# Attention scores from high and low parts of keys and queries, in products of 64 rows

## The chip, the core and the metric

The kernel runs on one core of a Trainium2 chip. Its time is that of one execution on the device in microseconds (us). The engines are TensorE (PE; its weight loads are listed apart as PEld), VectorE (DVE), ScalarE (ACT), GpSimd (POOL) and the queue that issues most transfers (SP). They run side by side and wait for one another through semaphores.

## What is computed

A layer with three parts runs on 8 batches of 64 rows of width 512. The first part is cross attention to a context of 1601 rows in 16 heads of width 32, with a "stablemax" in place of the softmax:

```python
def stablemax(x):
    s = jnp.where(x >= 0, x + 1.0, 1.0 / (1.0 - x))
    return s / jnp.sum(s, axis=-1, keepdims=True)
q = query @ Wq.T + bq          # and k, v from key_value
scores = jnp.einsum('bhqd,bhkd->bhqk', q, k) / np.sqrt(HD).astype(np.float32)
attn = stablemax(scores)
context = jnp.einsum('bhqk,bhkd->bhqd', attn, v)
```

Then come a causal self attention with 8 query heads and one key head, and a feed-forward part with 2 shared experts and 8 routed ones of which each row takes two. Each part adds its result to its input.

## The kernel before, in words

**Stages.** The cross attention takes most of the first 815 us. It goes batch by batch and in 104 chunks of keys, 13 to a batch: 12 of 128 keys and one of 65. The context comes in six parts to a batch (`PARTS`: five of 256 keys, one of 321), two chunks to a part and three to the last. Work is laid out by slots, one for each chunk (`for n in range(NSLOT)` in every engine's program). In a slot with an even number within its batch PE does the scores of two chunks (`group`), and then the weighted sums of the two before. In every slot it projects keys of the next part (two of its four blocks of 128 features, `keys`, L691) and the values of one chunk (`values`, L703). The self attention of finished pairs of batches ("tiles") is spread over these slots too (`STEPS`). The feed-forward part follows: shared experts to about 1015 us, then the routed ones.

**High and low parts.** The projections use fp32r operands: a value is rounded into a high part, the rest makes a low part, and three products (high by high, high by low, low by high) are summed in PSUM. The scores do not: `scores` (L719) multiplies the keys `kk` and queries `qc` in fp32, one product for each of four heads in a block g, over the 32 rows of the head: load `kk[r, ...]`, 32 rows by 128 keys, and move the 64 queries. Four products of a block lie on the four groups of 32 rows of the array and write four banks of `sc`.

**Buffers and order.** Projections take turns in two banks (`pj`). `take` lets PE write a bank only when `proj_read` says that DVE has read what lay there two uses ago. DVE's `keys` (L1234) adds the bias and stores a block, `values` (L1242) copies. DVE's order in an even slot: values of the slot before, first key block, weights of the first chunk, second key block; in the odd slot: values, weights of the second chunk, third and fourth key blocks.

**From scores to weights.** ACT reads the scores with Relu (L1133), then does Ln (L1140) and Exp (L1144); DVE's `weights` (L1247) adds the positive part, again from PSUM. POOL sums the weights for the denominators (L557) and makes the low parts of the context (L543). `weighted` (L732) multiplies weights and values in products of 128 rows by 32 columns; `denominators` (L744) sums over the rows.

**End of the stage.** SP loads the first expert weights (1 MB each, `load_shared`, L407) into a ring of buffers, three of them at slot NCH - 12, where NCH is 104; ACT rounds them (`weights_hi`, L1093), DVE makes the low part (L1338). `gelu` (L1100), `hidden` (L1347, L1349) and `shared_up` belong to the shared experts. The part's buffers (`sb1`) lie in the same memory as later ones, so that a ring buffer can be filled only when what lay there is done with.

Of the kernel before, what the change touches and what calls it, by code (L numbers as in the profile page):

```python
# [168 lines left out]
def build(nc, x, ctx0, ctx1, ctx2, ctx3, ctx4, ctx5, wq, bq, wk, bk, wv, bv, wo, bo, ak, av, aq, ap_, abp, rw, rb,  # L169
# [3 lines left out]
    with st:  # L173
# [17 lines left out]
        sd = sb("sd", [P, 4])  # L191
        rstd = sb("rstd", [P, 4])
# [60 lines left out]
        def sb1(name, shape, dt=F32):  # L253
# [9 lines left out]
        kk = sb1("kk", [P, 2, 4, WID])  # L263
        va = sb1("va", [P, VR, D])
        wqt = sb1("wqt", [P, 4, D])
        wot = wqt
        qc = sb1("qc", [P, 4, D])
        tt = sb1("tt", [P, TR, 1024])
        unit = sb1("unit", [P, 32])
# [14 lines left out]
        xBl = sb("xBl", [P, 4, 256], F32R)  # L284
        hh = sb("hh", [P, 4, D], F32R)
        hl = sb("hl", [P, 4, D], F32R)
        iota512 = sb("iota512", [P, D])
        sb("pad0", [P, 312])
        xr = sb("xr", [P, 2, D])
        GT = sb("GT", [P, 2, D], F32R)  # L290
        late_ring = [sb(f"ring{i}", [P, 2048]) for i in range(5, 8)]
        sb("pad1", [P, 32])
        ring = [sb(f"ring{i}", [P, 2048]) for i in range(3)] + early_ring + late_ring
        wsh, wsl = [sb("wsh0", [P, 2048], F32R), wsh1, wsh2], [sb("wsl0", [P, 2048], F32R), wsl1, wsl2]
        hr = sb("hr", [P, 2, D])
# [21 lines left out]
            "wkh_act wvh_act ch_act t_act ln_act ex_act rstd_act xt_act q_act "  # L317
            "exp_act xh_act gap_act wT_act ge_act wh_act rg_act yh_act "
            "pad_dve eps_dve iota_dve ones_dve wkl_dve wvl_dve cl_dve bqs_dve xr_dve proj_read f_dve "
# [49 lines left out]
        def weights_view(n, kn, hb):  # L369
            return tt[0:kn, n % TR, 512 * hb:512 * hb + 512].rearrange("p (h c) -> p h c", h=2)  # L370
# [12 lines left out]
        def sync(e):  # L383
# [31 lines left out]
            for n in range(NCH):  # L415
# [42 lines left out]

            e.wait_ge(s["v_pe"], NCH)
# [188 lines left out]
        def pe(e):  # L648
# [58 lines left out]
            def scores(n):  # L707
                i, k, kn = chunk(n)
                u, b, c0 = i % 2, i // NPT, 256 * (n - group_of(n)[0])
# [12 lines left out]

            def weighted(n):
# [6 lines left out]
                for g in range(4):  # L730
                    for h in range(4):
                        m = e.matmul(pob[b % 2][32 * h:32 * h + 32, 64 * g:64 * g + 64],  # L732
                                     va[0:kn, n % VR, P * g + 32 * h:P * g + 32 * h + 32],
                                     tt[0:kn, n % TR, 256 * h + 64 * g:256 * h + 64 * g + 64],
                                     start=(head and g == 0), stop=(tail and g == 3), skip_group_check=True)
                m.then_inc(s["p_pe"], 1)

            def denominators(b):
                dst = take("d", b)
                e.wait_ge(s["da_pool"], PER * b + PER)  # L740
                if b == 0:
                    e.wait_ge(s["unit_pool"], 1)
                for h in range(4):
                    m = e.matmul(dst[32 * h:32 * h + 32, 0:256], unit[:], dacc[:, b % 2, 256 * h:256 * h + 256],  # L744
                                 start=True, stop=True)
# [304 lines left out]
        def act(e):  # L1050
# [9 lines left out]

            def root(l, t):
# [62 lines left out]

            for n in range(NSLOT):
                for m in group(n):
# [4 lines left out]
                    e.wait_ge(s["s_pe"], group(n)[-1] + 1)  # L1131
                    for hb in range(2):
                        e.activation(weights_view(m, kn, hb), score_read(m, kn, hb), ACT.Relu,  # L1133
# [92 lines left out]
        def vector(e):  # L1226
            def keys(i, g):
# [16 lines left out]
            def weights(n, hb):  # L1244
                kn, t_ = chunk(n)[2], weights_view(n, chunk(n)[2], hb)
                e.wait_ge(s["ex_act"], 2 * n + hb + 1)
                e.scalar_tensor_tensor(t_, score_read(n, kn, hb), 0.0, t_, ALU.max, ALU.add).then_inc(s["f_dve"], 1)  # L1247
# [165 lines left out]
            e.tensor_copy(kio[:], iotai[:, P:P + 120].rearrange("p (k e) -> p k e", e=8)).then_inc(s["iota_dve"], 1)  # L1413
            values(0)
# [92 lines left out]
            for n in range(NSLOT):  # L1507
# [55 lines left out]
                for b, g, m in finished(n)[1]:  # L1563
                    normalised(b, g, m)

# [123 lines left out]
```

## Time and profile before

| what | us |
|---|---|
| median of 3 runs | 1291.81 (1291.58 to 1291.93) |
| the profiled execution's own time | 1291.71 |
| its span, from the first to the last instruction | 1290.0 |
| PE busy | 1278.1 |
| DVE busy | 640.0 |
| ACT busy | 625.2 |
| POOL busy | 405.8 |

The span is what the profile's rows add up to; the run's time has 1.7 us more around it. Busy times of engines overlap. In a row of the timeline the first number is the start in us from the span's start, the second the time to the end of the last of the merged instructions; "128*32" is rows by columns of the array that a product uses, and the shape after it is that of what is read. An fp32r operand that PE reads is listed as f32. An instruction's own duration holds its latency, so that durations of neighbours overlap: the pace of a row of instructions is read from their starts.

### The profile page before, as it was taken

Reading aid. Unit: us, or ns where it says so; the run is one execution under the profiler, and the core shown is the slowest. Engines: PE = TensorE matmul, PEld = TensorE weight load, DVE = VectorE, ACT = ScalarE, POOL = GpSimd, SP = SyncE. Lnnn points to the kernel's source line nnn. Section 1 sums busy time; section 2 is a strip of 40 time slices with the busy share of each in tenths; the row PEclk is TensorE's granted clock in tenths of the full one; section 3 lists DMA queues with packets and bytes.
Section 4 is the critical chain, followed back from the end, with each engine's and each line's share of the span. In section 5 each row is a group of like instructions: output and inputs, shape, how many; then the busy total and the mean of one; then the engine's idle time right before and its main releaser. Section 6 shows DMA issues by size and latency. Waiting matters only on the chain.

```text
span 1290.0 us, 31423 instructions
## 1 busy us (share of the span) xinstructions
PE 1278.1 (99%) x13820; PEld 1125.7 (87%) x13820; DVE 640.0 (50%) x971; ACT 625.2 (48%) x1093; POOL 405.8 (31%) x212
## 2 busy tenths in 40 slices
PE   8999999999999999999999999999999999999998
PEld 6898898888888889888889889798889999999897
DVE  5334443544443443443444454666776555565555
ACT  4445554544444544544543645647534444554443
POOL 1344444444444444444445435200032000100000
PEclk9999999999999999999999999999999999999999
DMA  6131111121111102121112031564566499999991
GB/s 221 61 109 34 35 38 35 34 71 53 48 63 35 46 27 99 35 74 39 35 38 100 23 127 63 237 254 164 171 193 202 151 334 352 360 343 332 359 392 39
DMA packets 34941, 174.98 MB, mean 136 GB/s; under 512 B 6184, under 2 KB 8392, under 8 KB 18544
## 3 DMA queue, kind: packets, MB, share of 16 engines
q1 hardware_dynamic: 33056, 168.16, 36.1%
q0 software_dynamic: 1744, 4.76, 1.1%
q8 instruction: 111, 1.82, 0.6%
q14 instruction: 30, 0.25, 0.1%
HBM read 166.84 MB, written 6.06 MB: 134 GB/s over the span
## 4 chain that ended last, share of the span: by engine, by line
PE 96%; DVE 2%; DMA 1%; ACT 0%; issue 0%; SPq 0%; DVEq 0%; ACTq 0%
PE bank L691 23%; PE bank L703 22%; PE bank L1017 11%; PE sc L1034 9%; PE sc L719 8%; PE sc L879 6%; PE bank L732 4%; PE bank L898 3%; PE sc L898 3%; PE bank L791 1%; PE bank L755 1%; PE bank L839 1%; DMA xres<-in_x 1%; PE bank L854 1%; PE sc L854 1%
## 5 line engine op out<-in xcount | busy, mean ns | idle before, releaser
L557 POOL TENSOR_TENSOR xn<-xn,tt 128x1024 f32<-128x1024 f32 x96 | 231.4, 2411 | 364.2 <-DVE tt L1247 363.9
L1133 ACT ACTIVATE tt<-sc 128x512 f32<-128x512 f32 (+1 forms) x208 | 108.0, 604 | 392.7 <-PE sc L719 392.7
L1338 DVE TENSOR_TENSOR wsl<-ring,wsh 128x2048 fp32r<-128x2048 f32 x72 | 167.7, 2330 | 113.3 <-ACT wsh L1093 113.1
L691 PE MATMUL bank<-cxh,wkh 128*128 128x256 f32 (+1 forms) x752 | 222.4, 296 | 1.0 <-DVE va L1242 1.0
L691 PE MATMUL bank<-cxl,wkh 128*128 128x256 f32 (+1 forms) x752 | 215.9, 287 | 0.4 <-issue 0.4
L691 PE MATMUL bank<-cxh,wkl 128*128 128x256 f32 (+1 forms) x752 | 215.1, 286 | 0.0
L1234 DVE TENSOR_SCALAR kk<-bank,bkt 128x256 f32<-128x256 f32 (+1 forms) x190 | 93.1, 490 | 202.1 <-PE bank L691 202.1
L703 PE MATMUL bank<-wvh,cxh 128*128 128x512 f32 (+1 forms) x416 | 164.5, 395 | 0.0
L703 PE MATMUL bank<-wvl,cxh 128*128 128x512 f32 (+1 forms) x416 | 163.8, 394 | 0.0
L703 PE MATMUL bank<-wvh,cxl 128*128 128x512 f32 (+1 forms) x416 | 162.8, 391 | 0.0
L1093 ACT CAST wsh<-ring 128x2048 fp32r<-128x2048 f32 x72 | 137.4, 1909 | 46.8 <-PE sc L1034 21.1
L1242 DVE COPY va<-bank 128x512 f32<-128x512 f32 (+1 forms) x104 | 71.8, 690 | 171.3 <-PE bank L703 171.3
L691 PEld LDWEIGHTS bank<-cxh,wkh 128*128 128x128 f32 x752 | 141.8, 189 | 11.0 <-issue 2.9
L1247 DVE SCALAR_TENSOR_TENSOR tt<-sc,tt 128x512 f32<-128x512 f32 (+1 forms) x208 | 133.3, 682 | 29.6 <-ACT tt L1144 29.6
L1017 PEld LDWEIGHTS bank<-xT,ring 128*128 128x128 f32 x1280 | 144.8, 192 | 1.0
L1017 PE MATMUL bank<-xT,ring 128*128 128x128 f32 x1280 | 144.8, 275 | 0.0
L691 PEld LDWEIGHTS bank<-cxl,wkh 128*128 128x128 f32 x752 | 141.9, 189 | 1.4
L691 PEld LDWEIGHTS bank<-cxh,wkl 128*128 128x128 f32 x752 | 142.3, 189 | 0.5 <-issue 0.5
L1140 ACT ACTIVATE tt<-tt 128x512 f32<-128x512 f32 (+1 forms) x208 | 121.6, 648 | 0.0
L1144 ACT ACTIVATE tt<-tt 128x512 f32<-128x512 f32 (+1 forms) x208 | 121.3, 645 | 0.0
L543 POOL TENSOR_TENSOR cxl<-ctxt,cxh 128x1024 fp32r<-128x1024 f32 (+1 forms) x47 | 108.3, 2305 | 27.5 <-ACT cxh L1059 27.5
L719 PEld LDWEIGHTS sc<-qc,kk 32*128 32x128 f32 (+1 forms) x3328 | 94.6, 182 | 20.2 <-issue 19.7
(257 smaller groups left out, 1965.4 us busy)
## 6 DMA issues: line engine op xcount, KB each, us to landing
ring<-in_w SPq DMA_DIRECT2D x112, 1024.0 KB, 7.2
ctxt<-in_ctx SPq DMA_DIRECT2D x40, 512.0 KB, 3.6
ctxt<-in_ctx SPq DMA_DIRECT2D x8, 642.0 KB, 4.0
wqt<-in_wo SPq DMA_DIRECT2D x4, 1024.0 KB, 6.5
wqt<-in_aq SPq DMA_DIRECT2D x4, 1024.0 KB, 6.2
wqt<-in_ap_ SPq DMA_DIRECT2D x4, 1024.0 KB, 5.7
yrows<-K SPq DMA_DIRECT2D x1, 2048.0 KB, 9.9
tt<-in_wk SPq DMA_DIRECT2D x2, 512.0 KB, 5.2
```

The source lines that it names most:

```text
L543: e.tensor_tensor(lo, src, hi.bitcast(F32), ALU.subtract).then_inc(s["cl_pool"], 1)
L557: e.tensor_tensor(dacc[0:kn, y, :], dacc[0:kn, y, :], tt[0:kn, w, :], ALU.add).then_inc(s["da_pool"], 1)
L691: m = e.matmul(dst[:, 0:n], (wkh, wkl)[a][:, c, g * P:(g + 1) * P], (cxh, cxl)[b][:, u, c, 0:n], start=(c == 0 and x_ == 0), stop=(c == 3 ...
L703: m = e.matmul(dst[0:kn, :], (cxh, cxl)[a][:, u, c, k * P:k * P + kn], (wvh, wvl)[b][:, c, :], start=(c == 0 and x_ == 0), stop=(c == 3 an ...
L719: m = e.matmul(sc[0:kn, h, c0 + 64 * g:c0 + 64 * g + 64], kk[r, u, g, k * P:k * P + kn], qc[r, g, 64 * b:64 * b + 64], start=True, stop=True)
L1017: m = e.matmul(bank[q % 2][:, P * jj:P * jj + P], ring[slot(un)][:, 512 * c + P * jj:512 * c + P * jj + P], xg[:, y, c, :], start=(c == 0) ...
L1034: m = e.matmul(bank[2][:], h_[:, j, :], w_[r_ % 3][:, 512 * jj:512 * jj + 512], start=(j == 0 and x_ == 0), stop=(j == 15 and x_ == 2))
L1093: e.copy(wsh[m % 3][:], ring[slot(un)][:]).then_inc(s["wh_act"], 1)
L1140: e.activation(tt[0:kn, w, r], tt[0:kn, w, r], ACT.Ln, bias=1.0).then_inc(s["ln_act"], 1)
L1144: e.activation(tt[0:kn, w, r], tt[0:kn, w, r], ACT.Exp, scale=-1.0).then_inc(s["ex_act"], 1)
L1247: e.scalar_tensor_tensor(t_, score_read(n, kn, hb), 0.0, t_, ALU.max, ALU.add).then_inc(s["f_dve"], 1)
L1338: e.tensor_tensor(wsl[m % 3][:], ring[slot(unit_split(m))][:], wsh[m % 3][:].bitcast(F32), ALU.subtract).then_inc(s["wl_dve"], 1)
```

## The change

The scores are made of three products with fp32r operands. The keys have a high part `kh` and a low part `kl`, both written by DVE from the same bank. The queries of a batch have `qh` and `ql` in block form: for a block of 128 features, a product takes 64 rows (two heads), and moves 128 columns, 64 for each of the two heads; the mask `own` makes the rows of the other head zero. Each of the two row halves writes a bank of its own, and each chunk has two banks. Four times (g) three terms times two halves makes 24 products a chunk. `qh` comes from ACT, `ql` from DVE, once for each batch, in slots ahead of it. Relu waits for its own chunk instead of the pair.

The new buffers take room in which expert weights were loaded early: the second shared load comes four slots later, the third behind the last scores; the layout of the rings, `hr` and `iota512` changes with it, and the first Gelu waits for the last weighted sum. The diff, cut to its core (the views of the columns in `weighted`, `denominators` and DVE's `weights` follow the new layout):

```diff
+        own = sb("own", [P, 2])
...
-        kk = sb1("kk", [P, 2, 4, WID])
+        kh = sb1("kh", [P, 2, 4, WID], F32R)
+        kl = sb1("kl", [P, 2, 4, WID], F32R)
...
+        qh = sb1("qh", [P, 2, 4, P], F32R)
+        ql = sb1("ql", [P, 2, 4, P], F32R)
...
-        def score_read(n, kn, hb):
-            c0 = 256 * (n - group_of(n)[0])
-            return sc[0:kn, 2 * hb:2 * hb + 2, c0:c0 + 256]
+        def weights_of(buffer, g, h):
+            c0 = 512 * (h // 2) + 128 * g + 64 * (h % 2)
+            return buffer[:, c0:c0 + 64]
+        def score_bank(n, hb):
+            return sc[:, 2 * (n - group_of(n)[0]) + hb, :]
...
                 if n == NCH - 12:
-                    for m in range(3):
-                        load_shared(m)
+                    load_shared(0)
+                if n == NCH - 8:
+                    e.wait_ge(s["ql_dve"], 2 * NB)
+                    load_shared(1)
...
+            e.wait_ge(s["s_pe"], NCH)
+            load_shared(2)
             e.wait_ge(s["v_pe"], NCH)
...
             def scores(n):
+                if n % PER == 0:
+                    e.wait_ge(s["ql_dve"], 2 * b + 2)
...
-                    for h in range(4):
-                        r = slice(32 * h, 32 * h + 32)
-                        m = e.matmul(sc[0:kn, h, c0 + 64 * g:c0 + 64 * g + 64], kk[r, u, g, k * P:k * P + kn],
-                                     qc[r, g, 64 * b:64 * b + 64], start=True, stop=True)
+                    for x_, (k_, q_) in enumerate(((kh, qh), (kl, qh), (kh, ql))):
+                        for j in range(2):
+                            r = slice(64 * j, 64 * j + 64)
+                            m = e.matmul(score_bank(n, j)[0:kn, P * g:P * g + P], k_[r, u, g, k * P:k * P + kn],
+                                         q_[r, b % 2, g, :], start=(x_ == 0), stop=(x_ == 2))
...
+            def queries(b, x_):
+                if b == 0 and x_ == 0:
+                    e.wait_ge(s["q_act"], 4)
+                    e.wait_ge(s["mk_dve"], 5)
+                if b >= 2 and x_ == 0:
+                    e.wait_ge(s["s_pe"], PER * (b - 1))
+                e.activation(qh[:, b % 2, :, 64 * x_:64 * x_ + 64], qc[:, :, 64 * b:64 * b + 64], ACT.Identity,
+                             scale=own[:, x_:x_ + 1]).then_inc(s["qh_act"], 1)
...
             def gelu(s_):
+                elif s_ == 0:
+                    e.wait_ge(s["p_pe"], NCH)
...
-                    e.wait_ge(s["s_pe"], group(n)[-1] + 1)
+                    e.wait_ge(s["s_pe"], m + 1)
...
+                b, x_ = divmod(n + 5, PER)
+                if 0 < b < NB and x_ < 2:
+                    queries(b, x_)
...
-                e.tensor_scalar(kk[:, u, g, 0:n], key_bank(i, g)[:, 0:n], bkt[:, g:g + 1], None,
-                                ALU.add).then_inc(s["proj_read"], 1)
+                e.tensor_scalar(kh[:, u, g, 0:n], key_bank(i, g)[:, 0:n], bkt[:, g:g + 1], None,
+                                ALU.add).then_inc(s["kh_dve"], 1)
+                e.wait_ge(s["kh_dve"], 4 * i + g + 1)
+                e.scalar_tensor_tensor(kl[:, u, g, 0:n], key_bank(i, g)[:, 0:n], bkt[:, g:g + 1],
+                                       kh[:, u, g, 0:n].bitcast(F32), ALU.add, ALU.subtract).then_inc(s["proj_read"], 1)
...
+            def queries_lo(b, x_):
+                e.wait_ge(s["qh_act"], 2 * b + x_ + 1)
+                e.scalar_tensor_tensor(ql[:, b % 2, :, 64 * x_:64 * x_ + 64], qc[:, :, 64 * b:64 * b + 64],
+                                       own[:, x_:x_ + 1], qh[:, b % 2, :, 64 * x_:64 * x_ + 64].bitcast(F32), ALU.mult,
+                                       ALU.subtract).then_inc(s["ql_dve"], 1)
...
+            e.memset(own[:], 0.0).then_inc(s["mk_dve"], 1)
+            e.wait_ge(s["mk_dve"], 1)
+            for h in range(4):
+                e.memset(own[32 * h:32 * h + 32, h % 2:h % 2 + 1], 1.0).then_inc(s["mk_dve"], 1)
...
                 for b, g, m in finished(n)[1]:
                     normalised(b, g, m)
+                b, x_ = divmod(n + 4, PER)
+                if 0 < b < NB and x_ < 2:
+                    queries_lo(b, x_)
```


## Rows read from the trace of the kernel before

**Rows 1.** The page: busy time of TensorE, and the chain that ended last by line:
```profile
PE 1278.1 (99%) x13820; PEld 1125.7 (87%) x13820; DVE 640.0 (50%) x971; ACT 625.2 (48%) x1093; POOL 405.8 (31%) x212
...
PE bank L691 23%; PE bank L703 22%; PE bank L1017 11%; PE sc L1034 9%; PE sc L719 8%; PE sc L879 6%; PE bank L732 4%; PE bank L898 3%; PE sc L898 3%; PE bank L791 1%; PE bank L755 1%; PE bank L839 1%; DMA xres<-in_x 1%; PE bank L854 1%; PE sc L854 1%
```

**Rows 2.** Attention stage: us, PE, PEld, DVE, ACT, POOL busy, clock, DMA share, GB/s:
```profile
37.00:815.00 778.00, 776.54 (x10412) 681.18 (x10408) 337.83 (x606) 381.77 (x728) 361.43 (x163) 1.00 0.16 54
```

**Rows 3.** The page's costliest groups, weight loads: busy us, mean ns of one:
```profile
L691 PEld LDWEIGHTS bank<-cxh,wkh 128*128 128x128 f32 x752 | 141.8, 189 | 11.0 <-issue 2.9
...
L1017 PEld LDWEIGHTS bank<-xT,ring 128*128 128x128 f32 x1280 | 144.8, 192 | 1.0
...
L719 PEld LDWEIGHTS sc<-qc,kk 32*128 32x128 f32 (+1 forms) x3328 | 94.6, 182 | 20.2 <-issue 19.7
```

**Rows 4.** Timeline of weight loads (start us, us, what), scores of two chunks:
```profile
404.15 1.88 PEld L719 LDWEIGHTS sc<-qc,kk 32*128 32x128 f32 x64 [0.35 <-issue]
406.09 0.94 PEld L732 LDWEIGHTS bank<-tt,va 128*32 128x32 f32 x64
```

**Rows 5.** The same, scores of a chunk with 65 keys:
```profile
417.14 0.56 PEld L719 LDWEIGHTS sc<-qc,kk 32*65 32x65 f32 x32 [0.36 <-issue]
```

**Rows 6.** Loads of fp32r operands in a row (L691), and loads in bf16 (L651):
```profile
407.12 0.19 PEld L691 LDWEIGHTS bank<-cxh,wkh 128*128 128x128 f32 x1
407.23 0.19 PEld L691 LDWEIGHTS bank<-cxl,wkh 128*128 128x128 f32 x1
...
407.59 0.19 PEld L691 LDWEIGHTS bank<-cxl,wkh 128*128 128x128 f32 x1
...
L651 PEld LDWEIGHTS bank<-ones x90: 95/98/151, 1.1 to 828.2; 128*128 128x128 bf16 x90
```

**Rows 7.** Products with 64 rows (L831): first four, and duration min/median/max:
```profile
340.90 0.45 PE L831 MATMUL bank<-xaT,V 64*64 64x256 f32 x4
...
L831 PE MATMUL bank<-xaT,V x32: 376/402/427, 340.9 to 885.0; 64*64 64x256 f32 x32
```

**Rows 8.** Operations of VectorE by themselves, and one beside GpSimd:
```profile
L1247 DVE SCALAR_TENSOR_TENSOR tt<-sc,tt x208: 675/680/693, 42.4 to 818.3; 128x512 f32<-128x512 f32 x96, 65x512 f32<-65x512 f32 x8
...
825.83 0.42 DVE L1356 COPY xT<-bank 128x256 f32<-128x256 f32 x1
...
828.87 0.42 DVE L1347 TENSOR_SCALAR hh<-hr 128x512 fp32r<-128x512 f32 x1
829.32 0.69 DVE L1349 SCALAR_TENSOR_TENSOR hl<-hr,hh 128x512 fp32r<-128x512 f32 x1
...
843.19 1.40 POOL L563 TENSOR_TENSOR xres<-xres,bpt 128x512 f32<-128x512 f32 x1 [20.49 <-DVE xa L1258]
...
843.48 1.66 DVE L1349 SCALAR_TENSOR_TENSOR hl<-hr,hh 128x512 fp32r<-128x512 f32 x1
```

**Rows 9.** Timeline of a regular part: VectorE, and TensorE's next use of the bank:
```profile
460.95 0.69 DVE L1242 COPY va<-bank 128x512 f32<-128x512 f32 x1 [1.41 <-PE bank L703]
...
462.75 0.47 DVE L1234 TENSOR_SCALAR kk<-bank,bkt 128x256 f32<-128x256 f32 x1
...
463.62 0.39 PE L703 MATMUL bank<-wvh,cxh 128*128 128x512 f32 x1
```

**Rows 10.** Timeline of GpSimd behind the weights:
```profile
411.33 2.41 POOL L557 TENSOR_TENSOR xn<-xn,tt 128x1024 f32<-128x1024 f32 x1 [8.99 <-DVE tt L1247]
```

**Rows 11.** End of the attention stage: TensorE, ScalarE, and landing of 1 MB (page):
```profile
814.18 0.70 PE L719 MATMUL sc<-qc,kk 32*65 32x64 f32 x32
...
819.64 0.65 PE L732 MATMUL bank<-tt,va 65*32 65x64 f32 x32
...
820.84 0.84 ACT L1100 ACTIVATE hr<-bank,b1s 128x256 f32<-128x256 f32 x2
821.57 1.91 ACT L1093 CAST wsh<-ring 128x2048 fp32r<-128x2048 f32 x1
...
wqt<-in_wo SPq DMA_DIRECT2D x4, 1024.0 KB, 6.5
```

More of the change, by code:

```diff
@@ L262, in build @@
         ctxt = sb1("ctxt", [P, 4 * WID])
-        kk = sb1("kk", [P, 2, 4, WID])
+        kh = sb1("kh", [P, 2, 4, WID], F32R)
+        kl = sb1("kl", [P, 2, 4, WID], F32R)
         va = sb1("va", [P, VR, D])
+        unit = sb1("unit", [P, 32])
         wqt = sb1("wqt", [P, 4, D])
@@ L267, in build @@
         qc = sb1("qc", [P, 4, D])
+        qh = sb1("qh", [P, 2, 4, P], F32R)
+        ql = sb1("ql", [P, 2, 4, P], F32R)
         tt = sb1("tt", [P, TR, 1024])
-        unit = sb1("unit", [P, 32])
         part1.close()
@@ L284, in build @@
         xBl = sb("xBl", [P, 4, 256], F32R)
+        ring2 = sb("ring2", [P, 2048])
         hh = sb("hh", [P, 4, D], F32R)
         hl = sb("hl", [P, 4, D], F32R)
-        iota512 = sb("iota512", [P, D])
-        sb("pad0", [P, 312])
+        hr = sb("hr", [P, 2, D])
+        sb("pad0", [P, 360])
         xr = sb("xr", [P, 2, D])
         GT = sb("GT", [P, 2, D], F32R)
+        ring1 = sb("ring1", [P, 2048])
+        iota512 = sb("iota512", [P, D])
         late_ring = [sb(f"ring{i}", [P, 2048]) for i in range(5, 8)]
-        sb("pad1", [P, 32])
-        ring = [sb(f"ring{i}", [P, 2048]) for i in range(3)] + early_ring + late_ring
+        ring = [sb("ring0", [P, 2048]), ring1, ring2] + early_ring + late_ring
         wsh, wsl = [sb("wsh0", [P, 2048], F32R), wsh1, wsh2], [sb("wsl0", [P, 2048], F32R), wsl1, wsl2]
-        hr = sb("hr", [P, 2, D])
         xh, xl = (xAh, xBh), (xAl, xBl)
@@ L316, in build @@
             "b2_pe hu_pe dn_pe ru_pe rd_pe sc_pe end_pe "
-            "wkh_act wvh_act ch_act t_act ln_act ex_act rstd_act xt_act q_act "
+            "wkh_act wvh_act ch_act t_act ln_act ex_act rstd_act xt_act q_act qh_act "
             "exp_act xh_act gap_act wT_act ge_act wh_act rg_act yh_act "
-            "pad_dve eps_dve iota_dve ones_dve wkl_dve wvl_dve cl_dve bqs_dve xr_dve proj_read f_dve "
+            "pad_dve eps_dve iota_dve ones_dve wkl_dve wvl_dve cl_dve bqs_dve xr_dve proj_read f_dve kh_dve ql_dve mk_dve "
             "cr_dve bn_dve xn_dve xa_dve xt_dve sm_dve nrm_dve xl_dve rt_dve hd_dve "
@@ L708, in scores @@
                 i, k, kn = chunk(n)
-                u, b, c0 = i % 2, i // NPT, 256 * (n - group_of(n)[0])
+                u, b = i % 2, i // NPT
+                if n % PER == 0:
+                    e.wait_ge(s["ql_dve"], 2 * b + 2)
                 if n >= 2:
@@ L733, in weighted @@
                                      va[0:kn, n % VR, P * g + 32 * h:P * g + 32 * h + 32],
-                                     tt[0:kn, n % TR, 256 * h + 64 * g:256 * h + 64 * g + 64],
-                                     start=(head and g == 0), stop=(tail and g == 3), skip_group_check=True)
+                                     weights_of(tt[0:kn, n % TR, :], g, h), start=(head and g == 0),
+                                     stop=(tail and g == 3), skip_group_check=True)
                 m.then_inc(s["p_pe"], 1)
@@ L742, in denominators @@
                     e.wait_ge(s["unit_pool"], 1)
+                dv = dacc[:, b % 2, :].rearrange("p (j g e q) -> p j g e q", j=2, g=4, e=2)
                 for h in range(4):
-                    m = e.matmul(dst[32 * h:32 * h + 32, 0:256], unit[:], dacc[:, b % 2, 256 * h:256 * h + 256],
-                                 start=True, stop=True)
+                    m = e.matmul(dst[32 * h:32 * h + 32, 0:256], unit[:], dv[:, h // 2, :, h % 2, :], start=True,
+                                 stop=True)
                 m.then_inc(s["d_pe"], 1)
@@ L1123, in act @@
                              scale=XSCALE).then_inc(s["q_act"], 1)
+            for x_ in range(2):
+                queries(0, x_)
             for n in range(NSLOT):
@@ L1130, in act @@
                         e.wait_ge(s["p_pe"], m - TR + 1)
-                    e.wait_ge(s["s_pe"], group(n)[-1] + 1)
+                    e.wait_ge(s["s_pe"], m + 1)
                     for hb in range(2):
-                        e.activation(weights_view(m, kn, hb), score_read(m, kn, hb), ACT.Relu,
+                        e.activation(tt[0:kn, m % TR, 512 * hb:512 * hb + 512], score_bank(m, hb)[0:kn, :], ACT.Relu,
                                      scale=-1.0).then_inc(s["t_act"], 1)
@@ L1244, in weights @@
             def weights(n, hb):
-                kn, t_ = chunk(n)[2], weights_view(n, chunk(n)[2], hb)
+                kn = chunk(n)[2]
+                t_ = tt[0:kn, n % TR, 512 * hb:512 * hb + 512]
                 e.wait_ge(s["ex_act"], 2 * n + hb + 1)
-                e.scalar_tensor_tensor(t_, score_read(n, kn, hb), 0.0, t_, ALU.max, ALU.add).then_inc(s["f_dve"], 1)
+                e.scalar_tensor_tensor(t_, score_bank(n, hb)[0:kn, :], 0.0, t_, ALU.max,
+                                       ALU.add).then_inc(s["f_dve"], 1)
+            def queries_lo(b, x_):
[3 more added lines that the diff above has]
+                                       ALU.subtract).then_inc(s["ql_dve"], 1)
             def stats_of(l, t):
@@ L1413, in vector @@
             e.tensor_copy(kio[:], iotai[:, P:P + 120].rearrange("p (k e) -> p k e", e=8)).then_inc(s["iota_dve"], 1)
+            for x_ in range(2):
+                queries_lo(0, x_)
             values(0)
```

2 lines of the change are left out of this document (removed).

## The prediction

> **What bounds the kernel now.** I read the page first: TensorE (PE) is busy in 99% of the span, and the chain that ended last is a list of PE lines, the scores (L719) among them with 8% [rows 1]. So what counts is how long PE's own queue gets, and any wait put into it. The table by stretches says where the change acts: the scores belong to the attention stage, 37 to 815 us, in which PE is idle for 1.5 us of 778; the clock granted there is 1.00, the upper of its two levels, 2.4 GHz [rows 2]. The groups by form then say what one score costs, and here the columns must be read with care: a product of fp32 operands stands in the trace as two instructions (3328 at L719, while the code issues 16 in each of 104 chunks), one of fp32r operands as one (L691 has 752 of each of three kinds, 188 blocks of 12) [rows 3]. And the mean of 182 ns is a latency, not a price: 64 such loads take 1.88 us together [rows 4].
>
> What sets that time? The weight loads themselves. Two chunks have 64 loads of 32 rows x 128 columns, in 16 rounds of four, one round to the four row groups of the array; the last of them starts 1.88 - 0.19 = 1.69 us after the first, so a round lasts 1.69/15 = 0.113 us [rows 4]. The chunk with 65 keys has loads of 65 columns: (0.56 - 0.13)/7 = 0.061 us a round [rows 5]; L732, with loads of 32 columns and the same moving side of 64 columns in fp32, (0.94 - 0.11)/15 = 0.055 us [rows 4]. Same products, three widths of load: the round follows the load's columns, down to the 0.055 us that the product itself takes. At 128 columns the load sets the pace. (If 0.113 were a load of 0.058 and a product of 0.055 in turn, 65 columns would give 0.084, not 0.061.)
>
> **The change, part by part.**
>
> *Score products.* Removed: 16 fp32 products a chunk (32 instructions, 8 rounds of four). Added: 4 column blocks x 3 terms x 2 row halves = 24 products of fp32r, each with a load of 64 rows x 128 columns and 128 moving columns; they come as 12 rounds of two. Needed are three prices that the trace does not show together.
> (a) The load in fp32r: L691's loads mean 189 ns against 192 for fp32 at L1017 [rows 3], and the second of a row of them starts 0.11 us after the first [rows 6]. I take the same 0.113 us; the bf16 loads of L651, 98 ns, show what a faster load would look like [rows 6].
> (b) Two halves of 64 rows side by side: at L831, products of 64 rows x 64 columns for two row halves and two column halves, the four first ones start within 0.45 - 0.43 = 0.02 us [rows 7]. So halves do overlap.
> (c) The product: 128 columns in fp32r, half of the 256 of L691 that follow at (407.59 - 407.12)/4 = 0.118 us, hence about 0.059 us, under the load's 0.113 [rows 6].
> So a round is 0.113 us again, and a chunk has 12 in place of 8. A batch has 12 full chunks and one of 65 keys: 96 x 4 x 0.113 = 43.4 us, and 8 x 4 x 0.061 = 2.0 us. Bounds of a round: from below 0.059, the product alone; from above 0.226, if the halves did not overlap. I take 0.113, since width, type and overlap each have a row of their own. The change lowers the passes of the array, but passes were not what set the pace.
>
> *Key blocks on DVE.* Each key block gets a second operation (the low part) after the first, behind a wait on DVE's own semaphore, and only then frees its bank of the two. Price: L1247, same form and also from PSUM, 0.68 us for 512 columns; the copies of 512 and of 256 columns (0.69, 0.42) give 0.27 us for 256 columns, so 0.41; the wait on itself is 0.03 us (828.87 + 0.42 to 829.32) [rows 8, 9]. Together 0.44 us x 192, 84 us of DVE work, covered wherever PE has the bank later. Where it has not: in a regular part DVE copies the values, does the weights twice, then the third key block, until 463.22; PE starts the values that need this bank at 463.62 [rows 9]. So 0.40 us are free, less the time of a release, and 0.44 come: I put 0.1 us of wait. Parts two to five of each batch have this pattern, 32 in all: 3.2 us. The first chunk's scores now end earlier relative to the second's and each chunk has banks of its own, so ACT starts no later; queued behind the late DVE is the fourth key block, which is due only with the next part's scores.
>
> *Low parts of the queries.* 16 operations on ACT and 16 on DVE (128x256). ACT has gaps. On DVE these read SBUF alone, and such an operation stands still while POOL works: L1349 took 1.66 us instead of 0.69 beside a POOL operation of 1.40 [rows 8]. One of the two per batch falls right behind a pair of weights, when POOL begins its 2.4 us of sums [rows 10]; I put 0.35 us of PE wait on each of 7 batches, 2.5 us. Bounds: 0, and 7 x 2.4 = 17 us. The first batch's pair stands ahead of the first values, where DVE has nothing else to do: 0.
>
> *Edits at about nothing.* The masks (five small memsets before the first data), the denominators with another order of columns (same 64 instructions), the weights as slices (same width), Relu waiting for one chunk instead of two. At the end of the stage: the third shared load moves behind the last scores, which end at 814.9; a load of 1 MB lands in 6.5 us, so at about 821.4, and ACT casts it at 821.57 [rows 11]: covered by about 0.2 us; if it is late, ACT's cast, DVE's split and the last normalisation behind it, which the last tile's output needs, move along, so 0 to 1 us. SP's queue behind it waits for the last values anyway. The first Gelu gets a wait for the last weighted sum, done at 820.29, and starts at 820.84 [rows 11]: 0, or 0.75 with a table load behind the wait.
>
> **Sum:** 43.4 + 2.0 + 3.2 + 2.5 = 51.1 us. The profiled execution took 1291.71 us, 1.7 over its span of 1290.0, and is 0.1 under the median of 1291.81. So 1342.8 us.
>
> **The rivals.**
> 1. *Loads stop being the limit (faster).* If an fp32r load of this shape were taken at bf16's rate, the product's 0.059 would set the round: 12 x 0.059 = 0.71 us against 0.90, so -0.194 x 96 = -18.7 us, +1.8 in the short chunks, +5.7 of waits: 1280.6 us. It decides from a round under 0.075 us. Against it: 189 ns for every fp32r load. The Trainium skill (TensorE: Matmul & The Clock Gate, weight-path perf modes) grants the fast weight load to 128 weights of any type but FP32; by that rule fp32r might have it. The trace disagrees: fp32r loads last as long as fp32 ones. 6%.
> 2. *Load and product of a row group take turns.* A round would be 0.113 + 0.059 = 0.172: 12 x 0.172 - 0.904 = 1.16 us x 96, +7.6, +5.7: 1416 us. Against it: the widths of rows 4 and 5, as worked out above, fit a product hidden under the load. The same page of the Trainium skill (Part 3, what overlaps and what doesn't) says that a load overlaps a running product only where the row group differs; those rows contradict it. 4%.
> 3. *Halves one after the other.* 24 loads x 0.113 = 2.71 us a chunk: +173.6, +7.8, +5.7: 1479 us. Against it [rows 7], though there the loads have 64 columns. 3%.
> 4. *DVE becomes the second bound.* If the low part is exposed in full in two blocks of each of 48 parts: 96 x 0.44 = 42 us in place of 5.7: 1379 us. For it: the 0.40 us that PE has to spare at that use is the whole reserve; against it: DVE is busy for 338 us of 778 [rows 2], and its order delays only the block behind the second pair of weights. 7%.
> 5. *Nothing measurable.* The round shortens to about 0.08 and the waits give it back: 1292 us, 1%.
>
> **How the numbers follow.** The forecast has 79%. Its own range: rounds of 0.107 to 0.118 (-2, +6), waits of 0 to 20 in place of 5.7: 1334 to 1363. To leave out 2 in 10 at most I go down to 1330 and up to 1372, half of the way that rival 4 opens. A measurement tells 0.2%, 2.6 us, from no change. Faster: rival 1, 0.06; same 0.01; slower: the rest, 0.93.
>
> **What would show it.** L719's line in the new trace: 2496 product rows, 24 a chunk, in 12 rounds at 0.11 us, a pair of full chunks in about 2.85 us instead of 1.94. The busy time of its loads near 140 us instead of 94.6 [rows 3]. The DVE line of the low part at 0.41 us, and a few us of PE waits released by it before L703. Wrong would be: rounds clearly off 0.11 us; a time under 1330, which needs a cheaper load; PE idle by more than 20 us in the stage.

## The result, and the profile after

The changed kernel takes 1347.65 us (1347.43 to 1349.17), the kernel before 1291.73 us beside it: ratio 1.0435, interval [1.0422, 1.0448], 55.9 us slower. The profiled execution has a span of 1345.8 us.

The page of the changed kernel, busy times and the chain by line, answers to [rows 1], and the stage's row of the table by stretches (us, PE, PEld, DVE, ACT, POOL busy, clock, DMA share, GB/s) to [rows 2]:

```profile
PE 1330.5 (99%) x12988; PEld 1171.4 (87%) x12988; DVE 745.3 (55%) x1184; ACT 635.9 (47%) x1109; POOL 403.8 (30%) x212
...
PE bank L712 21%; PE bank L700 20%; PE bank L1030 11%; PE sc L731 11%; PE sc L1047 8%; PE sc L892 6%; PE bank L744 4%; PE bank L911 3%; PE sc L911 3%; PE bank L804 1%; PE bank L768 1%; PE bank L852 1%; DVE tt L1282 1%; DMA xres<-in_x 1%; PE
```

```profile
37.00:862.00 825.00, 821.27 (x9504) 719.85 (x9505) 435.07 (x801) 387.87 (x737) 355.15 (x161) 1.00 0.15 49
```

PE is still the bound: its scores (L731) went from 8% to 11% of the chain. DVE's share of the chain rose from 2% to 4%, with its weights (L1282) now in the list. In the stage PE is idle for 3.7 us instead of 1.5; the busy time of DVE rose by 97 us, of which nearly all lies beside PE. Fewer instructions of PE take more time.

Weight loads of the scores alone, by stretches (us, PE busy, PEld busy, clock, DMA share, GB/s), first in the kernel before:

```profile
37.00:815.00 778.00, 101.98 (x3328) 94.29 (x3320) 1.00 0.16 54
```

and in the changed one:

```profile
37.00:862.00 825.00, 145.69 (x2472) 137.75 (x2472) 1.00 0.15 49
```

The time went there: 43.7 us more of products, 43.5 us more of loads. The timeline of loads shows the rhythm of the three terms, the answer to [rows 4]:

```profile
345.43 0.18 PEld L731 LDWEIGHTS sc<-qh,kh 64*128 64x128 f32 x2 [0.36 <-issue]
345.53 0.19 PEld L731 LDWEIGHTS sc<-qh,kl 64*128 64x128 f32 x2
345.64 0.19 PEld L731 LDWEIGHTS sc<-ql,kh 64*128 64x128 f32 x2
...
347.99 0.19 PEld L731 LDWEIGHTS sc<-ql,kh 64*128 64x128 f32 x2
```

From the second of the 24 rounds of two to the last, (347.99 - 345.53)/22 = 0.112 us. The rest is waits. PEld's waits (us, times, longest) of the changed kernel:

```profile
PEld sc L731 <- issue: 19.7, 52, 0.8
PEld bank L712 <- DVE kl L1268: 6.3, 27, 0.3
...
PEld bank L700 <- DVE va L1276: 4.0, 6, 0.8
```

The first line is the switch to the scores, with the same 19.7 us in both kernels; the second is new; the third was 1.7 us. Adding up TensorE's time from each start to the next by function gives: scores +44.6 us, key blocks +4.9, values +3.1, self attention's scores +2.0, the stretch ahead of the output stage's first product +0.9, the shared experts' first products +0.6, the rest under 0.1 each.

### The profile page after: what moved, and what is told of

Read it like the earlier page. It is cut to its first block, busy times and chain, and to the rows that moved or that the text cites. A ratio compares the mean times of both kernels' runs of the same rounds, so it can differ in the third digit from the quotient of the medians.

```text
span 1345.8 us, 29990 instructions
## 1 busy us (share of the span) xinstructions
PE 1330.5 (99%) x12988; PEld 1171.4 (87%) x12988; DVE 745.3 (55%) x1184; ACT 635.9 (47%) x1109; POOL 403.8 (30%) x212
## 4 chain that ended last, share of the span: by engine, by line
PE 94%; DVE 4%; issue 1%; DMA 1%; ACT 0%; SPq 0%; DVEq 0%; ACTq 0%
PE bank L712 21%; PE bank L700 20%; PE bank L1030 11%; PE sc L731 11%; PE sc L1047 8%; PE sc L892 6%; PE bank L744 4%; PE bank L911 3%; PE sc L911 3%; PE bank L804 1%; PE bank L768 1%; PE bank L852 1%; DVE tt L1282 1%; DMA xres<-in_x 1%; PE bank L867 1%
## 5 line engine op out<-in xcount | busy, mean ns | idle before, releaser
L1161 ACT ACTIVATE tt<-sc 128x512 f32<-128x512 f32 (+1 forms) x208 | 112.8, 594 | 427.7 <-PE sc L731 424.4
L1265 DVE TENSOR_SCALAR kh<-bank,bkt 128x256 fp32r<-128x256 f32 (+1 forms) x190 | 93.2, 491 | 216.2 <-PE bank L700 214.5
L712 PE MATMUL bank<-wvh,cxh 128*128 128x512 f32 (+1 forms) x416 | 167.7, 403 | 0.9
L1282 DVE SCALAR_TENSOR_TENSOR tt<-sc,tt 128x512 f32<-128x512 f32 (+1 forms) x208 | 132.8, 680 | 4.2 <-ACT tt L1172 4.0
L1168 ACT ACTIVATE tt<-tt 128x512 f32<-128x512 f32 (+1 forms) x208 | 119.6, 630 | 0.0
L1172 ACT ACTIVATE tt<-tt 128x512 f32<-128x512 f32 (+1 forms) x208 | 119.2, 626 | 0.0
L731 PE MATMUL sc<-qh,kh 64*128 64x128 f32 (+1 forms) x832 | 114.8, 275 | 0.1
```

Source lines behind the costliest of these rows:

```text
L712: m = e.matmul(dst[0:kn, :], (cxh, cxl)[a][:, u, c, k * P:k * P + kn], (wvh, wvl)[b][:, c, :], start=(c == 0 and x_ == 0), stop=(c == 3 an ...
L731: m = e.matmul(score_bank(n, j)[0:kn, P * g:P * g + P], k_[r, u, g, k * P:k * P + kn], q_[r, b % 2, g, :], start=(x_ == 0), stop=(x_ == 2))
L1161: e.activation(tt[0:kn, m % TR, 512 * hb:512 * hb + 512], score_bank(m, hb)[0:kn, :], ACT.Relu, scale=-1.0).then_inc(s["t_act"], 1)
L1168: e.activation(tt[0:kn, w, r], tt[0:kn, w, r], ACT.Ln, bias=1.0).then_inc(s["ln_act"], 1)
L1172: e.activation(tt[0:kn, w, r], tt[0:kn, w, r], ACT.Exp, scale=-1.0).then_inc(s["ex_act"], 1)
L1282: e.scalar_tensor_tensor(t_, score_bank(n, hb)[0:kn, :], 0.0, t_, ALU.max, ALU.add).then_inc(s["f_dve"], 1)
```

## The experiments

All ratios are to the kernel before, on the same chip as the run. Three groups: what sets the length of a round; what DVE's second operation costs; whether shorter loads could help the kernel before.

### What sets the length of a round

**after_two_terms**: the product of `kl` and `qh` is left out, and with it this part of the result.

```diff
-                    for x_, (k_, q_) in enumerate(((kh, qh), (kl, qh), (kh, ql))):
+                    for x_, (k_, q_) in enumerate(((kh, qh), (kh, ql))):
...
-                                         q_[r, b % 2, g, :], start=(x_ == 0), stop=(x_ == 2))
+                                         q_[r, b % 2, g, :], start=(x_ == 0), stop=(x_ == 1))
```

> The changed kernel without the product of the keys' low part by the queries' high part (that term is left out of the result; the low part is still made). Theory A (the time of the scores is the number of rounds times the load): 4 rounds fewer a chunk, 96 x 4 x 0.112 + 8 x 4 x 0.061 = 45 us less, about 1302.7 us, with 8 rounds a chunk as in the kernel before, and what stays over it (about 11 us) is the work on DVE and its waits. Rival D (DVE's second operation is the bound and PE only waits elsewhere): clearly less than 45 us gained, the gain turned into PE waits.

Measured: 1303.11 us, ratio 1.0086 [1.0069, 1.0103]. By starts, the scores take 98.5 us of TensorE's time instead of 142.9, as in the kernel before (98.4). Eight rounds of two fp32r loads cost what eight rounds of four fp32 loads cost. The 11 us above the kernel before are not scores.

**after_short_moves** and **after_narrow_loads** take one side of the product each, in terms two and three:

```diff
+                        w_ = P if x_ == 0 else 64
-                            m = e.matmul(score_bank(n, j)[0:kn, P * g:P * g + P], k_[...],
-                                         q_[r, b % 2, g, :], ...
+                            m = e.matmul(score_bank(n, j)[0:kn, P * g:P * g + w_], k_[...],
+                                         q_[r, b % 2, g, 0:w_], ...
```

```diff
+                        l_ = kn if x_ == 0 else min(kn, 96)
-                            m = e.matmul(score_bank(n, j)[0:kn, P * g:P * g + P], k_[r, u, g, k * P:k * P + kn],
-                                         q_[r, b % 2, g, :], start=(x_ == 0), stop=(x_ == 2))
+                            m = e.matmul(score_bank(n, j)[0:l_, P * g:P * g + P], k_[r, u, g, k * P:k * P + l_],
+                                         q_[r, b % 2, g, :], start=(x_ == 0), stop=True, skip_group_check=True)
```

> The changed kernel, in which the second and third term of every score product move the 64 columns of the first head of each pair instead of 128; all loads, the number of instructions and all waits stay. The low-part terms of the other head are left out of the result. Theory A, the weight load sets the length of a round: it stays at 0.112 us and the time at 1347.7 us, within 1.5. Rival B, the moving columns have a share in it (half of 128 fp32r columns is about 0.03 us less in 8 of 12 rounds of a chunk): 96 x 8 x 0.03 = 23 us less, about 1325; a pair of chunks in 2.4 us instead of 2.83.

> The changed kernel, in which the second and third term of every score product load 96 of the 128 keys of a full chunk; moving columns, number of instructions and waits stay. The low-part terms of the other 32 keys are left out of the result. Theory A, the load's columns set the length of a round: 0.084 us in place of 0.112 in 8 of the 12 rounds, 96 x 8 x 0.028 = 21.5 us less, about 1326; a pair of chunks in about 2.4 us. Rival B, something else does (the product, the supply of instructions, the handing over between two halves of the array): a round stays at 0.112 us and the time at 1347.7; in between, a round floor of 0.1 us would give about 1338.

Measured: half the moving columns 1349.26 us, 1.0438 [1.0422, 1.0454], 1.6 us above the changed kernel; 96 of 128 load columns 1327.7 us, 1.0279 [1.0263, 1.0295], 20 us less. The timeline of loads with 96 columns:

```profile
353.34 0.18 PEld L732 LDWEIGHTS sc<-qh,kh 64*128 64x128 f32 x2 [0.35 <-issue]
353.45 0.16 PEld L732 LDWEIGHTS sc<-qh,kl 64*96 64x96 f32 x2
353.54 0.17 PEld L732 LDWEIGHTS sc<-ql,kh 64*96 64x96 f32 x2
353.62 0.19 PEld L732 LDWEIGHTS sc<-qh,kh 64*128 64x128 f32 x2
```

Three rounds take 353.62 - 353.34 = 0.28 us, so 0.11 + 2 x 0.085: the round shrinks with the load's columns and with nothing else. With half the moving columns three rounds keep their 0.33 us:

```profile
346.43 0.19 PEld L732 LDWEIGHTS sc<-qh,kh 64*128 64x128 f32 x2 [0.36 <-issue]
...
346.76 0.19 PEld L732 LDWEIGHTS sc<-qh,kh 64*128 64x128 f32 x2
```

The 1.6 us more are not the scores: by starts these take 141.2 us instead of 142.9. A pair of chunks is 0.03 us shorter as a whole, where half the columns in 16 of its 24 rounds would have saved 0.48 us if each round had followed them (0.03 us a round, as expected for rival B). But in this profiled run TensorE's granted clock is at its lower level (0.50) in two stretches in which the changed kernel's profile has the upper one (us, busy times, clock, DMA share, GB/s):

```profile
238.70:242.00 3.30, 3.30 (x17) 3.30 (x17) 1.14 (x3) 3.30 (x8) 0.00 (x0) 0.50 0.00 0
859.90:863.20 3.30, 3.30 (x49) 2.68 (x39) 1.40 (x3) 3.30 (x8) 0.00 (x0) 0.50 0.00 0
```

At half the clock each costs 1.7 us: 2 x 1.7 - 1.7 = 1.7, the difference of the two times. What brought the clock down there isn't shown; PE was busy throughout.

That settles the scores: 0.112 us a round is the weight load, and the product lies under it.

### What the second operation costs

**after_no_low_keys**: DVE's low part of the keys isn't computed (`kl` is zero, set once); all 24 products of a chunk stay.

```diff
-                                ALU.add).then_inc(s["kh_dve"], 1)
-                e.wait_ge(s["kh_dve"], 4 * i + g + 1)
-                e.scalar_tensor_tensor(kl[:, u, g, 0:n], key_bank(i, g)[:, 0:n], bkt[:, g:g + 1],
-                                       kh[:, u, g, 0:n].bitcast(F32), ALU.add, ALU.subtract).then_inc(s["proj_read"], 1)
+                                ALU.add).then_inc(s["proj_read"], 1)
...
```

> The changed kernel without DVE's second operation per key block; the keys' low part is set to zero once, so its share is missing from the result, and all 24 products a chunk stay. Theory A: the second operation costs what the trace shows outside the scores, 28 waits of 0.2 us before values, 0.1 us after each for loads not taken ahead, three waits of 0.67 us behind the self attention's scores: 9 to 10 us less, about 1338 us. Rival D (DVE is the bound): 30 us and more less. Rival E (those waits come from the longer scores, not from the second operation): 1347 us.

Measured: 1336.62 us, 1.0344 [1.0327, 1.0361]: 11.0 us less than the changed kernel. The waits before the values are gone.

**before_second_op**: the kernel before, with a second operation of the same length that writes the same values again.

```diff
-                                ALU.add).then_inc(s["proj_read"], 1)
+                                ALU.add).then_inc(s["kh_dve"], 1)
+                e.wait_ge(s["kh_dve"], 4 * i + g + 1)
+                e.scalar_tensor_tensor(kk[:, u, g, 0:n], key_bank(i, g)[:, 0:n], bkt[:, g:g + 1],
+                                       kk[:, u, g, 0:n], ALU.add, ALU.max).then_inc(s["proj_read"], 1)
```

> The kernel before with a second operation on DVE for each key block, of the same size and with the same wait, that writes the same keys again (the larger of two equal values); the result is unchanged. Theory A: the same waits as in the changed kernel without its longer scores, 9 to 10 us more, about 1301.5 us. Rival E: 1292 us, as the waits need the longer scores.

Measured: 1300.91 us, 1.0067 [1.005, 1.0084], so +9.1 us. Loads before the values (busy us, mean ns, idle us and what ended it), here and without the low keys in the changed kernel:

```profile
L703 PEld LDWEIGHTS bank<-wvh,cxh 128*128 128x128 f32 (+1 forms) x416 | 76.4, 184 | 21.8 <-DVE kk L1237 6.2 <-issue 0.2
```

```profile
L712 PEld LDWEIGHTS bank<-wvh,cxh 128*128 128x128 f32 (+1 forms) x416 | 76.5, 184 | 15.6 <-issue 0.2
```

The operation brings 6.2 us of idle loads with it and takes them along when it goes. Why, a regular part of the changed kernel shows (VectorE, then the load and the products of the values):

```profile
477.56 0.68 DVE L1282 SCALAR_TENSOR_TENSOR tt<-sc,tt 128x512 f32<-128x512 f32 x1
...
478.15 0.47 DVE L1265 TENSOR_SCALAR kh<-bank,bkt 128x256 fp32r<-128x256 f32 x1
...
478.66 0.48 DVE L1268 SCALAR_TENSOR_TENSOR kl<-bank,bkt,kh 128x256 fp32r<-128x256 f32 x1
...
478.88 0.28 PE L700 MATMUL bank<-cxh,wkl 128*128 128x256 f32 x1
...
479.20 0.50 PE L712 MATMUL bank<-wvh,cxh 128*128 128x512 f32 x1
479.53 0.39 PE L712 MATMUL bank<-wvl,cxh 128*128 128x512 f32 x1
```

```profile
479.20 0.19 PEld L712 LDWEIGHTS bank<-wvh,cxh 128*128 128x128 f32 x1 [0.25 <-DVE kl L1268]
```

DVE is done with the third key block at 478.66 + 0.48 = 479.14, PE comes 0.06 us later. Without a wait it would have come 0.12 us after the product of 478.88, at 479.00: 0.20 us lost. And its load, which otherwise runs ahead under the product before, only starts now, so that the next product follows after 0.33 instead of 0.23 us: 0.10 us more. 27 such places x 0.30 = 8.1 us, the 4.9 + 3.1 of key blocks and values.

**after_keys_first**: DVE takes the third key block before the weights of the second chunk; nothing is left out.

```diff
+                for i, g in early:
+                    keys(i, g)
                 for m in group(n - 1)[1:]:
                     weights(m, 0)
                     weights(m, 1)
-                for i, g in early:
-                    keys(i, g)
```

> The changed kernel, in which DVE takes the third key block of a part before the weights of the part's second chunk, and not after them; nothing is left out. Theory A, the waits before the values come from DVE's order (third key block done only behind two sets of weights): 28 waits of 0.17 to 0.21 us go, and the load that wasn't taken ahead behind each (0.1 us) with them, about 8 us less: 1339.5. Rival B, the wait only moves: the weights of the second chunk come one key block later (0.97 us), and the weighted sums wait for them, time 1347.7 or more.

Measured: 1340.03 us, 1.037 [1.0354, 1.0386], 7.6 us less than the changed kernel. The same line of loads:

```profile
L712 PEld LDWEIGHTS bank<-wvh,cxh 128*128 128x128 f32 (+1 forms) x416 | 76.7, 184 | 16.7 <-DVE va L1276 0.9 <-issue 0.4
```

No wait for `kl` is left, against 6.3 us. Rival B appears only once, with PE waiting 0.5 us for weights. So it was DVE's order, not its load. It is the faster form of the changed kernel, and still 48 us slower than the kernel before.

**before_gelu_wait**: the kernel before, with `elif s_ == 0: e.wait_ge(s["p_pe"], NCH)` ahead of the first Gelu.

> The kernel before, in which the first Gelu gets the changed kernel's wait for the last weighted sum, and nothing else. Theory A, the load of the function table stands behind that wait on ACT, so that the first Gelu comes about 0.5 to 0.8 us later and the output stage with it: 1292.5 us. Rival B, the table is loaded ahead of the wait, or the output stage waits for something else: 1291.8, no difference.

Measured: 1292.51 us, 1.0003 [0.9994, 1.0013]: in the time nothing that can be told. In the trace the mechanism is plain. ScalarE's table load and the output stage's first product in the kernel before, with the wait, and in the changed kernel:

```profile
819.54 1.28 ACT L1100 ACT_TABLE_LOAD   x1
...
829.01 1.55 PE L755 MATMUL bank<-wqt,xT 128*128 128x512 f32 x3 [0.50 <-DVE xT L1371]
```

```profile
820.92 1.28 ACT L1102 ACT_TABLE_LOAD   x1 [0.88 <-PE bank L732]
...
830.26 1.12 PE L755 MATMUL bank<-wqt,xT 128*128 128x512 f32 x2 [1.22 <-DVE xT L1373]
```

```profile
875.27 1.28 ACT L1125 ACT_TABLE_LOAD   x1 [0.84 <-PE bank L744]
...
884.62 1.55 PE L768 MATMUL bank<-wqt,xT 128*128 128x512 f32 x3 [1.22 <-DVE xT L1413]
```

The table load stands behind the wait (ScalarE is idle for 0.88 and 0.84 us ahead of it, and not at all in the kernel before), and the output stage's first product waits for 1.22 us in both, against 0.50 us in the kernel before: 0.7 us.

### Shorter loads in the kernel before

If the load's columns set the pace, the kernel before should gain from loads of half the columns. **before_half_loads** cuts every score product into two halves of the keys:

```diff
-                    for h in range(4):
-                        r = slice(32 * h, 32 * h + 32)
+                    for k0, k1 in ((0, 64), (64, kn)):
+                        for h in range(4):
+                            r = slice(32 * h, 32 * h + 32)
...
+                            m = e.matmul(sc[k0:k1, h, ...], kk[r, u, g, k * P + k0:k * P + k1],
```

> The kernel before with each fp32 score product cut in two along the keys: loads of 64 columns for two halves of the output's partitions, same queries, same bank; nothing left out. Theory A (the load of 128 columns sets the pace of the scores, and loads for different column halves run side by side): 8 rounds of eight at about 0.061 us in place of 8 rounds of four at 0.113, so 96 x 8 x 0.052 = 40 us less, about 1252 us, a pair of chunks in 1.1 us. Rival B (what sets the pace is one load after another in a row group, whatever its columns): 16 rounds of 0.061 a chunk, 0.98 us instead of 0.90, about 1299 us. Rival C (the products' moving data sets the pace): about 1292 us or more.

Measured: 1331.78 us, 1.0304 [1.0287, 1.0321], a clear miss: far above theories A and B, and theory C ("1292 us or more") has the products no faster, which they are. The products of two chunks do take 1.59 us instead of 2.01. Their first groups of eight instructions follow each other in 0.058 us by their starts, near the 0.061 of theory A; from the 33rd of the 128 instructions on the mean distance is 0.0114 us, 0.09 us for eight. And behind them:

```profile
423.78 1.00 PE L720 MATMUL sc<-qc,kk 32*64 32x64 f32 x74
424.71 1.08 PE L733 MATMUL bank<-tt,va 128*32 128x64 f32 x58
427.21 0.31 PE L733 MATMUL bank<-tt,va 128*32 128x64 f32 x6 [1.42 <-issue]
```

and over the whole kernel (waits of PE: us, times, longest):

```profile
PE bank L733 <- issue: 22.2, 14, 4.4
PE bank L691 <- issue: 17.8, 11, 4.3
```

PE stands still without waiting for a semaphore, behind the 128 instructions of 64 half products (fp32, two instructions each) and up to some 60 of sums in a row. I read it as instructions that come too slowly, and the records of DMA packets bear this out. Queue q8 of the page, first in the kernel before, then here:

```profile
q8 instruction: 111, 1.82, 0.6%
```

```profile
q8 instruction: 137, 2.24, 0.7%
```

It has 26 packets of 16384 bytes more, and PE has 3328 product instructions and as many loads more: 6656 / 26 = 256 instructions a packet, so this queue brings PE's program. Of PE's 26 stops over 0.25 us that end with "issue" (40.3 us), every one ends 1.1 to 1.6 us behind the landing of such a packet, though packets land only every 3 to 18 us there: the stop shown above ends at 427.21, the packet landed at 425.70. And from one stop to the next PE has run 127 product instructions or a multiple of it, within three: a packet or a whole number of them, with the loads and a few instructions of other kinds. PE waits for its next instructions. Behind five of the stops the granted clock is also at its lower level for a while, which costs some 8 us beside the stops, as this stretch shows:

```profile
835.20:838.60 3.40, 3.40 (x15) 3.40 (x14) 0.80 (x2) 3.40 (x7) 0.00 (x0) 0.51 0.02 5
```

To give the packets more time I moved the long products of the key blocks between the two bursts, first alone as a control (**before_sums_later**), then with the halves (**half_loads_sums_later**), then with halves in two of four column blocks only, and none in the chunks of 65 keys (**half_loads_two_blocks**):

```diff
-                for m in group_before(n):
-                    weighted(m)
+                late_sums = n < NCH and early + late
+                if not late_sums:
+                    for m in group_before(n):
+                        weighted(m)
...
+                if late_sums:
+                    for m in group_before(n):
+                        weighted(m)
                 if values_in(n) is not None:
```

> The kernel before with the weighted sums of the two earlier chunks moved behind the key blocks of the slot, on PE alone; nothing left out. Every theory: PE does the same work in another order, 1291 to 1293 us. It is the control for the next two.

> Score products cut in two along the keys as in before_half_loads, with the weighted sums moved behind the key blocks, so that 128 and 64 short products no longer follow each other. Theory F (the half loads do work, 1.52 us a pair instead of 1.94, and the 46 us lost were PE standing without instructions after 192 short products in a row): the idle time of PE with nothing to wait for goes away, 1291.8 - 48 x 0.42 = about 1272 us. Rival G (the instructions cannot be supplied on average, or the clock fell): about 1320 to 1332 us again.

> The same with only two of the four column blocks cut in two, and not in the chunk of 65 keys: 96 short products for a pair of chunks instead of 128. Theory A, load pace: 4 rounds of 0.061 and 4 of 0.113 a chunk, 0.70 us instead of 0.90, so 20 us less if no instruction is missing: about 1272 us. Theory F expects it near or under half_loads_sums_later, since bursts are shorter. Rival G: gains half of nothing, 1290 to 1310 us.

| kernel | us | ratio |
|---|---|---|
| before_sums_later | 1303.45 | 1.0089 [1.0073, 1.0106] |
| half_loads_sums_later | 1305.79 | 1.0109 [1.0092, 1.0126] |
| half_loads_two_blocks | 1309.82 | 1.0141 [1.0124, 1.0158] |

With long products between the bursts the stops fall from 40.0 us (the two lines of waits above) to

```profile
PE bank L733 <- issue: 7.9, 5, 2.5
```

All three sums were wrong, though (1309.8 us lies just inside rival G's 1290 to 1310, but not for its reason: 0.8 us of stops are left in that run). The control missed: moving the sums costs 11.5 us by itself. The move puts two more changes between products of the whole array and products of a part of it into a slot. By the starts, a slot is 0.18 us longer for it, in 53 places, and 1.5 us more are three waits of the denominators for DVE's `xa`. In the second, the scores take 89.1 us instead of 98.4, and not the half, and the sums, with the stops that are left, take back as much: against its control it is 2.3 us slower. (A chunk of 65 keys becomes products of 64 keys and of 1.) In the third the scores take 103.1 us: the mixture is dearer than the whole loads alone. Its starts say why. Four groups of eight half loads at 0.058 us and four rounds of whole ones at 0.112 would make 1.36 us a pair of chunks, and from the first start to the last there are 1.84. Each change from halves to wholes costs 0.18 us more than the pace, each one back 0.16, and a pair has three inside.

What is shown is that the stops end with an instruction packet. What sets when a packet is asked for, and why instructions inside a burst follow at 0.011 us once the first 32 are through, stays open.

## Why the prediction was right

Forecast 1342.8 us in 1330 to 1372, measured 1347.65 us: the direction, the mechanism and the size hold, and the forecast is 4.9 us short.

- **The round of loads** (0.113 us, 43.4 + 2.0 us): 0.112 us, +44.6 us. The step from three widths of load to "the load sets the pace" is shown by **after_narrow_loads** and **after_short_moves**, the 12 rounds in place of 8 by **after_two_terms**. Loads busy near 140 us were forecast: 137.75. Pair of chunks in 2.85 us: 2.83.
- **The low part on DVE** was mis-sized, and is the one term that was well off: 3.2 us of waits were forecast, some 8 came. Of the three figures behind "0.1 us of wait", two were short. The operation takes 0.484 us, not 0.41, as long as the `kh` operation ahead of it (0.479) and not as the difference of two copies had it:

```profile
L1268 DVE SCALAR_TENSOR_TENSOR kl<-bank,bkt,kh 128x256 fp32r<-128x256 f32 x158 | 76.5, 484 | 5.6
```

  With the wait on itself it adds 0.51 to 0.52 us, and the release 0.06 us: 0.52 + 0.06 - 0.40 = 0.18, beside the 0.20 us seen. The reload of 0.10 us behind each wait was in no step. The place itself (values, behind two sets of weights) was right, and so nearly was the number of places: 27 of the 32.
- **The low part of the queries**: 2.5 us forecast. 3 places of self attention's scores give 2.0 us. There the operation stands still beside POOL, as the step said (1.93 us, against a median of 0.484), and holds up the copy of the values, for which PE waits:

```profile
331.41 2.40 POOL L566 TENSOR_TENSOR xn<-xn,tt 128x1024 f32<-128x1024 f32 x1 [11.56 <-DVE tt L1282]
...
332.16 1.93 DVE L1287 SCALAR_TENSOR_TENSOR ql<-qc,own,qh 128x256 fp32r<-128x256 f32 x1
...
334.02 0.68 DVE L1276 COPY va<-bank 65x512 f32<-65x512 f32 x1
...
334.75 0.39 PE L700 MATMUL bank<-cxh,wkh 128*128 128x256 f32 x1 [0.56 <-DVE va L1276]
```

  The size was near by luck: other places than the seven that were priced made it, and without the low part of the keys (**after_no_low_keys**) only 0.5 us of it is left, so the two terms belong together.
- **The first Gelu**: 0 was taken, the other end (0.75, a table load behind the wait) came: 0.7 us by the traces. The third shared load was covered: the second cast follows the first Gelu at once in both kernels.

Together: 44.6 + 8.0 + 2.0 + 0.7 = 55.3 of 55.9 us. The forecast, 51.1, had 45.4 + 3.2 + 2.5 + 0. One slip stands in its range: rounds of 0.107 us in all 12 rounds would be 96 x 12 x 0.006 = 6.9 us less, not 2, so that its own lower end was 1330, the bound that it went down to in any case.

The rivals: **1** (cheaper fp32r loads) falls with 0.112 us, the pace of fp32 loads. The Trainium skill (TensorE: Matmul & The Clock Gate, weight-path perf modes) keeps the fast load from FP32 alone; by these rows fp32r hasn't got it either, or not in this form. **2** and **3** would have given rounds of 0.17 and 0.226 us; halving the moving columns would have shortened the former. The same page of the Trainium skill (Part 3), by which a load overlaps a running product only where the row group differs, isn't what these rows show: each round loads the same two row halves as the one before, at the load's own pace. What the same part says ahead of that list fits them: there a load may also go ahead when it targets the background weight buffer. **4** was half a step away: the same order of DVE that it names set the waits, but 0.30 us at 27 places instead of 0.44 at 96. **5** (no change) falls with the 55.9 us.

## What to carry to other kernels

Where products are short, count the weight loads and their columns, not the passes: a scheme with more products of a cheaper type loses if each brings a load as wide. Cutting the loads shorter makes more instructions and more changes of shape, and here both ate the gain. Before adding an operation to an engine that is half idle, find the one use of a buffer with the least slack and price it in full: the operation, its wait on itself, the release, and the load that isn't taken ahead behind a wait. If it doesn't fit, change the order first: one block moved forward took the 8 us of waits out, for 7.6 us of time.

## What was not expected of the hardware

- Behind some 190 short products and as many loads in a row PE stood still for up to 4.4 us, 40 us in all, until 1.1 to 1.6 us behind the landing of a 16 KB packet of its instructions; within the burst of 128 it starts one only every 11 ns on the mean, after a first group at 7 ns.
- Two more changes between products of the whole array and of a part of it made a slot 0.18 us longer (**before_sums_later**). The Trainium skill (TensorEngine Tiling, Key Properties) says that changing the tiling mode drains TensorE, without a figure; the control run agrees and has one.
- Changes between halved loads and whole ones in one chunk cost 0.16 to 0.18 us each, so that the mixture (103.1 us for the scores) was slower than whole ones alone (98.4), while loads of 96 and 128 columns mixed in **after_narrow_loads** ran at the pace of their columns. That 64 columns are a tile of another shape and 96 are not would fit; widths between weren't tried.
- The load of an activation table isn't done during a wait that stands ahead of the activation: it starts behind it, here after 0.88 us in which ScalarE is idle, and the output stage came 0.7 us late by it.
